# Causal mask of the by-query scores by 64x64 identities on four quarters of the array, and by-query scores one pair further ahead

## The chip, the cores and the metric

The kernel runs on one core of a Trainium2 chip. The metric is the device time of one execution in microseconds (us). "Before" is the median of three runs.

## What is computed

A batch of 16 sequences with 256 rows of 128 channels goes through two layers. Each has attention and a feed-forward part, and a layer norm behind each of the two. The change concerns the attention of the second layer:

```python
q = (x @ Wq).reshape(B, T, HEADS, D_K).transpose(0, 2, 1, 3)      # 16 heads of 8
k = (x @ Wk).reshape(B, T, HEADS, D_K).transpose(0, 2, 1, 3)
v = (x @ Wv).reshape(B, T, HEADS, D_V).transpose(0, 2, 1, 3)      # 64 per head
scores = jnp.einsum('bhqd,bhkd->bhqk', q, k) / scale
causal = jnp.triu(jnp.ones((T, T), dtype=bool), k=1)
scores = jnp.where(causal, -jnp.inf, scores)
attn = jax.nn.softmax(scores, axis=-1)
out = jnp.einsum('bhqk,bhkd->bhqd', attn, v) ... @ Wo
```

## The kernel before

The second layer (`l1_layer`) is one block in which each engine has its own program, a loop over `step(b)` for b from -4 to 17, unrolled. The engines meet only by semaphores. The order of the work in each program is written out by hand; each call such as `context(b, 0)` first waits for what it needs and then issues its instructions. The 16 heads of a sequence are handled as 8 pairs (`PRE = 8`); the two heads of a pair, u = 0 and 1, have their queries and keys on rows 0 to 63 and 64 to 127 of the stacks `q_ring` and `k_ring`.

Scores are computed twice. `scores_by_query(b, c)` puts queries on the partitions of the PSUM tensor `by_query` (one bank for each u), and VectorE's `maxima(b, c)` reduces them to the negated maximum of each query (L1375); after four pairs it combines them (L1380). `maxima_by_head` turns the maxima by two small transposes on TensorE, ScalarE's `maxima_out` copies them to `max_rows`, and SyncE's `rows_to_stack` writes them as one more row into `q_ring`, where they are subtracted by the matmul itself. `scores_by_key(b, c)` waits for that row at c = 0 and 4, and puts keys on the partitions of `by_key`. ScalarE's `exponential` makes probabilities of them (L1250), GpSimd's `mask` zeroes those above the diagonal (L1447), and `context` and `denominators` sum them on TensorE. `by_query` has room for one pair: `scores_by_query(b, c)` waits until `max_done` shows that the pair before it has been reduced.

Since the maximum must not see keys after the query, the by-query scores carry their own causal mask. Before the scores, a matmul with an identity of 128x128 adds a constant, `causal`, which holds -1e30 above the diagonal, to the two diagonal blocks of the bank (L1113). The scores follow with L1117 and L1121.

A step of TensorE has eight blocks, separated by blank lines in the code. Each has by-key scores of one pair, the context of the pair two before it, some other work (transposes of x, queries and keys, values, denominators, projections), and last by-query scores of the next sequence. I call them block 1 to block 8. The programs of ScalarE, VectorE and GpSimd follow the same rhythm. Names that matter here:

- `x_by_channel` (L1085), `queries_keys` (L1092), `values_of` (L1103), `maxima_by_head` (L1136), `context` (L1166), `denominators` (L1179) and `project` (L1190) on TensorE.
- `high_part` (L1263) on ScalarE: the first of three bf16 parts of queries and keys. `load_slots` (L113, L115) on SyncE copies the parts into the stacks, 12 loads a sequence, and `rows_to_stack` comes behind them in SyncE's queue.
- `reciprocals` (L1387), `add_attention`, `add_expert`, `second_input`, `third_input` (L1336) and `divide` (L1393) on VectorE. `second_input` waits for `root(pow2, ...)` on GpSimd, which waits for the statistics of `add_expert`.
- `root` (L1439, L1441), `low_part`, `gather` on GpSimd.

## Time and profile before

| | |
|---|---|
| median of 3 runs | 949.31 us (949.01, 949.31, 952.53) |
| profiled execution | 950.26 us, its span 948.5 us |
| TensorE clock granted, whole span | 0.937 |
| TensorE matmul, busy | 790.8 us, 83% of the span |
| VectorE / ScalarE / GpSimd, busy | 575.1 / 472.5 / 296.2 us |
| one step of the second layer, 605 to 631 us | TensorE 25.54 of 26.00 us, VectorE 17.75, ScalarE 12.87, GpSimd 10.91; granted clock 1.00 |

The second layer's scores run from about 406 to 811 us. Times are microseconds from the start of the span. A weight load (PEld) overlaps the matmuls (PE) of the same engine, and the ends of matmuls are modelled, so the recorded times of neighbours overlap.

### The profile page before, as it was taken

What the parts mean: (1) busy time and instruction counts of PE and PEld (TensorE: products, weight loads), DVE (VectorE), ACT (ScalarE), POOL (GpSimd) and SP (SyncE); (2) the same over time, 40 slices, a digit from 0 to 9 for tenths busy, and PEclk for the clock granted to TensorE, in tenths of its full rate; (3) what the DMA queues carried; (4) which work ended last, traced back from release to release, by engine and by line L of the source; (5) the groups of instructions that cost most, each with busy time, mean ns of one, the idle gap of its engine ahead of it and who ended that gap; (6) DMA issues with size and microseconds to landing.
All of it is one profiled execution on the core that took longest, in us unless ns stands there. A gap on an engine that the chain in (4) does not pass through costs nothing. (4 is left out here: it accounts for less than half of the span.)

```text
span 948.5 us, 19520 instructions
## 1 busy us (share of the span) xinstructions
PE 790.8 (83%) x7061; PEld 451.7 (48%) x7061; DVE 575.1 (61%) x1715; ACT 472.5 (50%) x750; POOL 296.2 (31%) x437
## 2 busy tenths in 40 slices
PE   1588989998829999179999999999999999739970
PEld 0234444444316778125555555555555555534430
DVE  4458999999531111244576776666666656324687
ACT  0377888887812222035454545445455444306664
POOL 3012333333336000424344444434443322100152
PEclk9989999999958999679999999999999999878995
DMA  0274333433215553221454444333334332210002
GB/s 26 72 239 124 97 89 96 108 84 89 69 32 129 158 149 88 67 59 45 96 96 96 96 96 92 74 86 78 81 76 96 79 85 51 56 45 0 1 0 89
DMA packets 111705, 78.02 MB, mean 82 GB/s; under 512 B 12272, under 2 KB 103088, under 8 KB 111616
## 3 DMA queue, kind: packets, MB, share of 16 engines
q1 hardware_dynamic: 107984, 71.16, 30.5%
q0 software_dynamic: 3344, 5.56, 2.2%
q8 instruction: 53, 0.87, 0.4%
q14 instruction: 36, 0.29, 0.1%
q10 hardware_dynamic: 288, 0.13, 0.1%
HBM read 37.86 MB, written 13.63 MB: 54 GB/s over the span
## 5 line engine op out<-in xcount | busy, mean ns | idle before, releaser
L1375 DVE TENSOR_REDUCE l_neg_max<-l_by_query 128x6 bf16<-128x768 f32 x128 | 122.5, 957 | 129.9 <-PE l_by_query L1121 129.6
L1447 POOL TENSOR_SCALAR_AFFINE_SELECT l_probs<-l_probs 128x512 f32<-128x512 f32 x128 | 87.1, 680 | 190.9 <-ACT l_probs L1250 190.7
L493 ACT ACTIVATE l_probs<-l_ps_s,minus_bound 128x1024 f32<-128x1024 f32 x128 | 137.9, 1116 | 2.3 <-PE l_ps_s L367 1.4
L1250 ACT ACTIVATE l_probs<-l_by_key 128x768 f32<-128x768 f32 x128 | 103.8, 811 | 68.1 <-PE l_by_key L1151 63.9
L1166 PE MATMUL l_ps_c<-l_probs,l_values 128*64 128x256 f32 (+1 forms) x1024 | 113.5, 343 | 0.0
L1166 PEld LDWEIGHTS l_ps_c<-l_probs,l_values 128*64 128x64 f32 x1024 | 62.9, 138 | 39.7 <-issue 21.2
L1190 PE MATMUL l_ps_v<-w_o,l_ctx 128*128 128x128 f32 x512 | 68.6, 290 | 15.1 <-DVE l_ctx L1393 15.1
L382 PE MATMUL l_ps_o<-l_probs,l_vpad 128*32 128x256 f32 x1024 | 80.6, 397 | 0.2
L1103 PE MATMUL l_ps_v<-w_v,l_xT 128*128 128x512 f32 x128 | 72.8, 651 | 0.4 <-ACT l_values L1271 0.2
L1190 PEld LDWEIGHTS l_ps_v<-w_o,l_ctx 128*128 128x128 f32 x512 | 62.6, 200 | 20.9 <-DVE l_ctx L1393 15.5
L1271 ACT ACTIVATE l_values<-l_ps_v 128x512 f32<-128x512 f32 x64 | 38.2, 597 | 65.4 <-PE l_ps_v L1103 60.0
L1393 DVE TENSOR_TENSOR l_ctx<-l_ctx,l_rrep 128x512 f32<-128x512 f32 x64 | 46.8, 774 | 23.9 <-DMA l_rrep<-rden_d 22.2
L1113 PE MATMUL l_by_query<-causal,ident_bf 128*128 128x256 bf16 x256 | 50.4, 279 | 12.2 <-DMA k_ring<-l_parts 10.0
L940 ACT ACTIVATE ex_hT<-ex_ps_h 128x640 f32<-128x640 f32 x32 | 22.5, 704 | 70.0 <-PE ex_ps_h L911 70.0
L1179 PE MATMUL l_ps_d<-l_probs,sums 128*32 128x256 f32 (+1 forms) x1024 | 55.1, 333 | 0.0
L367 PE MATMUL l_ps_s<-q_ring,k_ring 64*128 64x256 bf16 x512 | 51.5, 280 | 2.6 <-ACT l_probs L493 1.5
L1113 PEld LDWEIGHTS l_by_query<-causal,ident_bf 128*128 128x128 bf16 x256 | 21.6, 98 | 59.2 <-issue 33.2
L926 PE MATMUL ex_ps_y<-w,ex_hT 128*128 128x128 f32 (+1 forms) x384 | 48.9, 280 | 0.0
L776 POOL DMA_INDIRECT disp_d<-l_x,l_sidx x32 | 32.5, 1015 | 51.1 <-DVE weight L653 46.3
L926 PEld LDWEIGHTS ex_ps_y<-w,ex_hT 128*128 128x128 f32 (+1 forms) x384 | 43.4, 173 | 3.2 <-issue 0.2
L1277 ACT ACTIVATE l_ctx<-l_ps_c 128x512 f32<-128x512 f32 x64 | 38.2, 597 | 10.6 <-PE l_ps_c L1166 10.6
L911 PE MATMUL ex_ps_h<-ex_xeT,w 128*128 128x320 f32 x128 | 40.6, 463 | 1.3 <-DVE ex_xeT L960 0.7
(229 smaller groups left out, 1422.5 us busy)
## 6 DMA issues: line engine op xcount, KB each, us to landing
l_rrep<-rden_d SPq DMA_DIRECT2D x32, 512.0 KB
q_ring<-l_parts SPq DMA_DIRECT2D x192, 64.0 KB
k_ring<-l_parts SPq DMA_DIRECT2D x192, 64.0 KB
w<-in_L_ffn_w_dram SPq DMA_DIRECT2D x32, 256.0 KB, 3.0
disp_d<-zeros SPq DMA_DIRECT2D x8, 320.0 KB, 3.7
l_xin<-in_L_attn_x_dram SPq DMA_DIRECT2D x16, 128.0 KB, 3.1
l_xr<-in_L_attn_x_dram SPq DMA_DIRECT2D x16, 128.0 KB, 2.5
x_d<-l_x SPq DMA_DIRECT2D x16, 128.0 KB, 2.1
```

Source lines behind the costliest of these rows:

```text
L367: last = pe.matmul(ps_s[c % 2][:, g * N:(g + 1) * N], k_ring[i][half, 2 * j + e, kb * P:(kb + 1) * P], q_ring[i][half, 2 * j + e, :], star ...
L382: last = pe.matmul(ps_o[32 * g:32 * g + 32, t * N:(t + 1) * N], vpad[p][:, kb, f:f + 32], probs[c % RING][:, g * N:(g + 1) * N], start=u = ...
L493: act.activation(probs[c % RING][:, :], ps_s[c % 2][:, :], ACT.Exp, bias=k["minus_bound"][:, :], scale=SCALE).then_inc(probs_sb, 1)
L926: last = pe.matmul(ps_y[p][0:n, t // P * C:(t // P + 1) * C], hT[p][:, f, t:t + n], w2_sb[q][:, f, :], start=f == 0, stop=f == FC - 1)
L1103: pe.matmul(ps_v[:, :], xT[b % 2][:, j * P:(j + 1) * P], w_v[:, half * 512:(half + 1) * 512], start=True, stop=True).then_inc(v_ps, 1)
L1113: pe.matmul(by_query[:, u, P:3 * P], ident_bf[:, :], k["causal"][:, 0:2 * P], start=True, stop=False, skip_group_check=True)
L1166: last = pe.matmul(ps_c[u * DV:(u + 1) * DV, c % 2, q0:N], values[b % 2][:, kb, h * DV:(h + 1) * DV], pr[:, u, first:first + N - q0], star ...
L1179: last = pe.matmul(ps_d[32 * g:32 * g + 32, q0:N], sums[:, j, :], probs[(2 * j + e) % P_RING][:, u, first:first + N - q0], start=j == 0 an ...
L1190: last = pe.matmul(ps_v[:, j * C:(j + 1) * C], ctxs[b % 2][:, i, j * P:(j + 1) * P], w_o[:, i, :], start=i == 0, stop=i == PAIRS - 1)
L1250: act.activation(probs[c % P_RING][:, :, 0:N + P], by_key[:, :, 0:N + P], ACT.Exp, scale=SCALE).then_inc(p_sb, 1)
L1375: dve.tensor_reduce(neg_max[:, :, half, :, h].rearrange("p a u -> p u a"), by_query[:, :, 0:3 * P].rearrange("p u (a q) -> p u a q", a=3), ...
L1447: pool.affine_select(out=corners, in_=corners, compare_op=ALU.is_ge, fill=0.0, base=0, pattern=[[0, 4], [1, P]], channel_multiplier=-1).th ...
```

## The change

The constant `causal` becomes `corner`, 256 columns wide; each half of its partitions holds the first 64 rows of a causal block twice. The mask of a pair is now four matmuls, each with a 64x64 identity on its own quarter of the array. Two cover queries 0 to 63 of both diagonal blocks with 256 columns, one for each u; two cover queries 64 to 127, for which only keys 64 to 127 of a block need the mask, with 128 columns. The second two use the row half of the other u.

All by-query scores move one pair further ahead, in all programs: block 1 now does pair 2 of the next sequence where it did pair 1, and blocks 7 and 8 do pairs 0 and 1 of the one after. With them `x_by_channel` moves from the head of block 1 to behind its context, `maxima_by_head(b + 1, 0)` from block 5 to block 4, `high_part` behind `exponential(b, 4)`, and the work of VectorE and GpSimd is placed anew: on VectorE `add_expert` goes behind `maxima(b + 1, 4)` and `second_input` behind `maxima(b + 1, 5)`; on GpSimd `root(pow2, ...)` goes behind `mask(b, 6)` and `gather` behind `mask(b, 7)`.

```diff
-            pool.memset(k["causal"][:, :], 0.0).then_inc(filled, 1)
+            pool.memset(k["corner"][:, :], 0.0).then_inc(filled, 1)
...
-            pool.affine_select(out=k["causal"][:, :].rearrange("p (a b) -> p a b", b=P),
-                               in_=k["causal"][:, :].rearrange("p (a b) -> p a b", b=P),
-                               compare_op=ALU.is_ge, fill=-1e30,
-                               base=0, pattern=[[0, 4], [-1, P]], channel_multiplier=1).then_inc(cut, 1)
+            pool.wait_ge(cut, 2)
+            for half in range(2):
+                rows = k["corner"][64 * half:64 * half + 64, :].rearrange("p (a b) -> p a b", b=P)
+                pool.affine_select(out=rows, in_=rows, compare_op=ALU.is_ge, fill=-1e30,
+                                   base=0, pattern=[[0, 2], [-1, P]], channel_multiplier=1).then_inc(cut, 1)
...
                     for u in two:
-                        pe.matmul(by_query[:, u, P:3 * P], ident_bf[:, :], k["causal"][:, 0:2 * P],
+                        r = slice(64 * u, 64 * u + 64)
+                        pe.matmul(by_query[0:64, u, P:3 * P], ident_bf[r, r], k["corner"][r, :],
+                                  start=True, stop=False, skip_group_check=True)
+                    for u in two:
+                        r = slice(64 - 64 * u, 128 - 64 * u)
+                        later = by_query[64:128, u, P:3 * P].rearrange("p (a k) -> p a k", k=P)[:, :, 64:P]
+                        pe.matmul(later, ident_bf[r, r], k["corner"][r, :].rearrange("p (a k) -> p a k", k=P)[:, :, 0:64],
                                   start=True, stop=False, skip_group_check=True)
...
             def step(b):
-                x_by_channel(b + 2)
                 scores_by_key(b, 2)
                 context(b, 0)
-                scores_by_query(b + 1, 1)
+                x_by_channel(b + 2)
+                scores_by_query(b + 1, 2)
 
                 scores_by_key(b, 3)
                 context(b, 1)
                 denominators(b, 0)
                 queries_keys(b + 2)
-                scores_by_query(b + 1, 2)
+                scores_by_query(b + 1, 3)
 
                 scores_by_key(b, 4)
                 context(b, 2)
                 values_of(b + 1, 0)
-                scores_by_query(b + 1, 3)
+                scores_by_query(b + 1, 4)
 
                 scores_by_key(b, 5)
                 context(b, 3)
                 denominators(b, 1)
+                maxima_by_head(b + 1, 0)
                 values_of(b + 1, 1)
-                scores_by_query(b + 1, 4)
+                scores_by_query(b + 1, 5)
 
                 scores_by_key(b, 6)
                 context(b, 4)
-                maxima_by_head(b + 1, 0)
                 values_of(b + 1, 2)
-                scores_by_query(b + 1, 5)
+                scores_by_query(b + 1, 6)
 
                 scores_by_key(b, 7)
                 context(b, 5)
                 denominators(b, 2)
                 values_of(b + 1, 3)
-                scores_by_query(b + 1, 6)
+                scores_by_query(b + 1, 7)
 
                 scores_by_key(b + 1, 0)
                 context(b, 6)
                 project(b - 1, 0)
-                scores_by_query(b + 1, 7)
+                scores_by_query(b + 2, 0)
 
                 scores_by_key(b + 1, 1)
                 context(b, 7)
                 denominators(b, 3)
                 project(b - 1, 1)
                 maxima_by_head(b + 1, 1)
-                scores_by_query(b + 2, 0)
+                scores_by_query(b + 2, 1)
 
             steps(step)
 
                     act.activation(max_rows[half][:, :], turned, ACT.Copy).then_inc(rows_sb, 1)
 
             def step(b):
+                exponential(b, 2)
                 x_out(b + 2)
-                exponential(b, 2)
 
                 exponential(b, 3)
                 context_out(b, 0)
+
+                exponential(b, 4)
                 high_part(b + 2)
-
-                exponential(b, 4)
                 values_out(b + 1, 0)
 
                 exponential(b, 5)
                 context_out(b, 1)
+                maxima_out(b + 1, 0)
                 values_out(b + 1, 1)
 
                 exponential(b, 6)
-                maxima_out(b + 1, 0)
                 values_out(b + 1, 2)
 
                 exponential(b, 7)
 
             def step(b):
                 reciprocals(b - 1)
+                maxima(b + 1, 2)
+
                 add_attention(b - 2)
-                maxima(b + 1, 1)
+                maxima(b + 1, 3)
+
+                lower_parts(b + 2)
+                third_input(b - 2)
+                maxima(b + 1, 4)
 
                 add_expert(b + 3)
-                maxima(b + 1, 2)
-
-                third_input(b - 2)
-                lower_parts(b + 2)
-                maxima(b + 1, 3)
+                maxima(b + 1, 5)
 
                 second_input(b + 3)
-                maxima(b + 1, 4)
-
                 divide(b - 1, 0)
                 divide(b - 1, 1)
-                maxima(b + 1, 5)
+                maxima(b + 1, 6)
 
                 divide(b - 1, 2)
                 divide(b - 1, 3)
-                maxima(b + 1, 6)
-
                 maxima(b + 1, 7)
+
                 maxima(b + 2, 0)
+
+                maxima(b + 2, 1)
 
             steps(step)
 
 
             def step(b):
                 mask(b, 2)
+                mask(b, 3)
                 root(pow3, x3_step, (b - 2) * X3 + 1 + 2 * NB, mv3, veps3, rstd3, b - 2)
-                mask(b, 3)
-                root(pow2, x2_step, (b + 3) * X2 + 3 * NB, mv2, veps2, rstd2, b + 3)
                 mask(b, 4)
                 low_part(b + 2)
                 mask(b, 5)
+                mask(b, 6)
+                root(pow2, x2_step, (b + 3) * X2 + 3 * NB, mv2, veps2, rstd2, b + 3)
+                mask(b, 7)
                 gather(b + 4)
-                mask(b, 6)
-                mask(b, 7)
                 mask(b + 1, 0)
                 mask(b + 1, 1)
 
```

## Rows read from the trace of the kernel before

**Rows 1.** Line L1387 in 477 to 785 us: count, durations, first and last start.
```profile
L1387 DVE RECIPROCAL l_rden<-l_ps_d x13: 1747/1748/1750, 475.7 to 783.2; 128x256 f32<-128x256 f32 x13
```

**Rows 2.** Groups by line and form, 477 to 785 us: busy us, mean ns | idle before.
```profile
L1148 PEld LDWEIGHTS l_by_key<-q_ring,k_ring 64*128 64x128 bf16 x192 | 9.3, 94 | 8.2 <-DMA q_ring<-l_max_rows 5.5 <-issue 1.8
```

**Rows 3.** Waits of TensorE's matmuls, 470 to 790 us: total, times, longest.
```profile
PE l_by_query L1113 <- DVE l_neg_max L1375: 1.6, 2, 1.1
```

**Rows 4.** Timeline, step of 603 us: start, us, what [idle before <-releaser].
```profile
602.14 0.09 PEld L1136 LDWEIGHTS l_ps_m<-ident_bf,l_neg_max 128*8 128x8 bf16 x2
602.34 0.11 PEld L1113 LDWEIGHTS l_by_query<-causal,ident_bf 128*128 128x128 bf16 x2
...
602.94 0.20 PEld L1085 LDWEIGHTS l_ps_m<-ident,l_x 128*128 128x128 f32 x2 [0.16 <-issue]
...
603.58 0.87 PE L1166 MATMUL l_ps_c<-l_probs,l_values 128*64 128x256 f32 x8
...
604.38 0.11 PEld L1113 LDWEIGHTS l_by_query<-causal,ident_bf 128*128 128x128 bf16 x2 [0.17 <-issue]
...
604.71 0.10 PEld L1117 LDWEIGHTS l_by_query<-k_ring,q_ring 63*128 63x128 bf16 x2 [0.21 <-issue]
...
605.94 0.59 PEld L1179 LDWEIGHTS l_ps_d<-l_probs,sums 128*32 128x32 f32 x16 [0.17 <-issue]
```

**Rows 5.** Timeline of TensorE's matmuls, 612.5 to 614.3 us.
```profile
612.55 1.12 PE L1103 MATMUL l_ps_v<-w_v,l_xT 128*128 128x512 f32 x2
613.51 0.38 PE L1113 MATMUL l_by_query<-causal,ident_bf 128*128 128x256 bf16 x2
613.83 0.28 PE L1117 MATMUL l_by_query<-k_ring,q_ring 63*128 63x256 bf16 x2
...
614.00 0.27 PE L1148 MATMUL l_by_key<-q_ring,k_ring 64*128 64x256 bf16 x2
```

**Rows 6.** Timeline of the first two context matmuls at 603.58 us.
```profile
603.58 0.44 PE L1166 MATMUL l_ps_c<-l_probs,l_values 128*64 128x256 f32 x2
```

**Rows 7.** Matmuls by line and form, 477 to 785 us.
```profile
L1166 PE MATMUL l_ps_c<-l_probs,l_values 128*64 128x256 f32 x388 | 63.3, 405 | 0.0
```

**Rows 8.** Timeline of TensorE's matmuls, 616.6 to 621 us.
```profile
616.72 0.28 PE L1148 MATMUL l_by_key<-q_ring,k_ring 64*128 64x256 bf16 x2
...
619.97 0.22 PE L1121 MATMUL l_by_query<-k_ring,q_ring 63*128 63x128 bf16 x2
```

**Rows 9.** Timeline of ScalarE, 607 to 618 us.
```profile
607.90 0.60 ACT L1263 ACTIVATE l_parts<-l_ps_m 128x512 bf16<-128x512 f32 x1 [1.24 <-PE l_ps_m L1092]
...
608.56 0.81 ACT L1250 ACTIVATE l_probs<-l_by_key 128x768 f32<-128x768 f32 x1
...
617.10 0.81 ACT L1250 ACTIVATE l_probs<-l_by_key 128x768 f32<-128x768 f32 x1
```

**Rows 10.** Timeline of GpSimd, 609 to 618 us.
```profile
609.01 0.22 POOL L1439 TENSOR_SCALAR l_veps<-l_mv 128x2 f32<-128x2 f32 x1 [0.39 <-DVE l_mv L1330]
...
609.31 0.74 POOL L1441 TENSOR_TENSOR l_rstd<-l_veps,minus_half 128x2 f32<-128x2 f32 x1
...
617.97 0.64 POOL L1447 TENSOR_SCALAR_AFFINE_SELECT l_probs<-l_probs 128x512 f32<-128x512 f32 x1 [0.57 <-ACT l_probs L1250]
```

**Rows 11.** Timeline of VectorE, 391 us and 616 to 620 us.
```profile
391.85 0.60 DVE L1336 TENSOR_SCALAR l_x<-l_y,l_mv,l_rstd 128x128 f32<-128x128 f32 x2 [1.17 <-POOL l_rstd L1441]
...
616.21 1.74 DVE L1393 TENSOR_TENSOR l_ctx<-l_ctx,l_rrep 128x512 f32<-128x512 f32 x2 [1.03 <-DMA l_rrep<-rden_d]
617.87 0.95 DVE L1375 TENSOR_REDUCE l_neg_max<-l_by_query 128x6 bf16<-128x768 f32 x1
...
618.74 1.28 DVE L1393 TENSOR_TENSOR l_ctx<-l_ctx,l_rrep 128x512 f32<-128x512 f32 x2
```

**Rows 12.** Timeline of SyncE's issues: the first stack load of a step.
```profile
609.49 0.58 SPq L113 DMA_DIRECT2D q_ring<-l_parts  x1
```

**Rows 13.** Timeline at the layer's start: the first by-key scores.
```profile
421.70 0.28 PE L1148 MATMUL l_by_key<-q_ring,k_ring 64*128 64x256 bf16 x2 [2.13 <-DMA q_ring<-l_max_rows]
```

More of the change, by code:

```diff
@@ L178, in _ @@
             s.did(dve.tensor_copy(k["gate_T"][:, :], gps[:, :]))
-            dve.wait_ge(cut, 3)
+            dve.wait_ge(cut, 4)
             s.did(dve.tensor_copy(k["ident_bf"][:, :], k["ident"][:, :]))
@@ L1882, in program @@
             "tri_bf": sb("tri_bf", [P, P], BF16), "ones_bf": sb("ones_bf", [P, P], BF16),
-            "ones": sb("ones", [P, P], FP32), "causal": sb("causal", [P, 4 * P], BF16),
+            "ones": sb("ones", [P, P], FP32), "corner": sb("corner", [P, 2 * P], BF16),
             "zeros": sb("zeros", [P, 5 * C], FP32), "minus_half": sb("minus_half", [P, 4], FP32),
```

## The prediction, made before the change was run

> **What bounds the kernel now.** I read the page first, then the second layer alone: the waits of TensorE, the timeline of one step, and the same timeline for each other engine. The layer is a loop of 16 steps. The reciprocals, one a step, start from 475.7 to 783.2 us, 13 of them, so a step takes 307.5 / 12 = 25.63 us [rows 1]. TensorE works through all of it at a granted clock of 1.00, its upper level of 2.4 GHz (table above). Its only real idle times are the by-key scores that wait for the row of maxima in `q_ring`, 5.5 us in these 12 steps or 0.46 a step [rows 2], and two waits for a reduction of VectorE, 1.6 us together [rows 3]. (Most of what is booked before L1113 on the weight-load row is a load that waits while a matmul still streams, and costs nothing.) So the step is TensorE's instruction time, 25.17 us, plus 0.46 us of waiting; a microsecond on TensorE or in that wait is a microsecond of the kernel, 12 to 16 times over.
>
> Inside TensorE's time there is a second thing to see: the price of changing the tile shape. After the values' matmuls, which like the mask use the whole array, the first mask matmul starts at 613.51, 0.16 us before the recorded end of the work before it (612.55 + 1.12) [rows 5]. After the context's matmuls, whose tiles are 128x64, the mask's weight load starts at 604.38, only 0.07 us before their recorded end (603.58 + 0.87) [rows 4]. A change of shape thus drains the array: 0.10 us, with the exposed weight load 0.11. Every change shows it, also that from the transposes of 8 columns to the mask (0.20 us for two tiny matmuls, 602.14 to 602.34) and that from the by-query scores to the transposes of x (the 0.16 before 602.94) [rows 4].
>
> **The change on TensorE.** *The mask.* Today, after a change of shape, its two matmuls and the drain behind them take 604.38 to 604.71, 0.33 us [rows 4]. Four quarter matmuls are not in this trace, so I bound them. The nearest row is the context, whose two 128x64 tiles run at once: the first two matmuls are recorded with 0.44 us together, 0.43 each, the mean of that form is 0.405 over two such and two behind a hidden load, so the latter take 0.38 and a load of 64 columns shows for 0.05 [rows 6, 7]. A 256-column bf16 matmul streams for 0.11: the two of the mask take 613.51 to 613.83 with one drain of 0.10 in it [rows 5]. If the four quarters run together the mask takes 0.05 + 0.11 + 0.10 of drain = 0.26 us: 0.07 less, eight times a step, -0.56 us. Lower bound: no drain between 64x64 and the by-query scores' 64x128, 0.16 us. Upper bound: nothing overlaps, 0.32 of streaming + 0.15 = 0.47 us. I take 0.26, as for the context's tiles.
>
> The Trainium skill, "TensorEngine Tiling (Array Packing)", Key Properties, says that changing the tiling mode, not just the tile, drains the TensorE; the trace agrees with its 0.10 us. The same page, PSUM Pressure, says that different row tiles cannot access one PSUM bank simultaneously. Here each bank gets its second quarter from the other row half; by that rule the 128-column quarters come after the 256-column ones, which is the third case below.
>
> *The changes of shape.* In blocks 2 to 7 of a step the mask follows values, projections or queries and keys, all on the whole array, with no change of shape. With 64x64 tiles each gains one: 6 x 0.11. In block 8 the transposes before it drain already: no new one. In block 1 the transposes of x no longer stand between by-query and by-key scores, which have one shape, but between context and mask: two changes go, one comes, -0.11. Together +0.54 us a step. So what the mask saves (-0.56) the drains take back: 0.0 us a step, and this is the core of the forecast. The half-size constant and the one more select at the start move tenths of a microsecond, once.
>
> **The change in the order.** Everything VectorE and GpSimd do for TensorE must be placed again. I follow one step from T, the first by-key matmul of block 5.
>
> TensorE: blocks 5 and 6 take 614.00 to 620.02 today (by-key follows the by-query matmuls of 619.97 at once) [rows 5, 8], 6.02 us. The transposes of the maxima leave block 5 for block 4 (-0.20 [rows 4]), two changes of shape less two shorter masks come (+0.08): 5.90. Mask and scores of pair 7 are the last 0.26 + 0.18 of it, so TensorE asks for `max_done` of pair 6 at T + 5.46.
>
> The other engines: pair 6's reduction now stands behind `second_input` and two `divide`s, `second_input` behind `root(pow2)` on GpSimd, and that behind `mask(b, 6)`. By-key to exponential 0.38 (616.72 to 617.10), exponential 0.81, hand-over 0.06, mask 0.64 [rows 8, 9, 10]; root 1.04 (609.01 to 610.05) and a hand-over, 1.09 [rows 10]: T + 2.98. Two normalisations take 0.60 (391.85) where GpSimd runs nothing beside them, as here: 3.6. Two `divide`s with a mask beside them, as `mask(b, 7)` will be, 1.74 (616.21), alone 1.28 (618.74); I take 1.7: 5.3. The reduction 0.95 and a hand-over 0.05 [rows 11]: T + 6.3. TensorE waits **0.8 us** (0.4 if the `divide`s run alone, 1.2 if the normalisations too lose 0.4 to a mask). Today `second_input` runs two blocks after its statistics and no such chain ends at TensorE. Behind the waiting mask are queued the by-key scores of the next batch's pair 0, and with them ScalarE and GpSimd; `divide` 2 and 3 end at about T + 7.7, before the projection asks at T + 7.8.
>
> This wait does not add to the wait for the row; it covers it. That row is issued behind 12 stack loads, which SyncE begins at 609.49 [rows 12], and those wait for the high part. `high_part` now comes after exponential 4: 608.56 + 0.81 + 0.60 [rows 9], less 0.13 that TensorE is earlier there, is 609.84, where today it is there before 609.49. So the row is 0 to 0.4 us later (less where a load is held by the queue anyway). The earlier transposes of the maxima don't help: it is SyncE's queue that is late, not `max_rows`. The wait of a step becomes the larger of 0.8 and 0.46 + (0 to 0.4); as the row's own wait spreads from 0 to over 1 us, I take 0.92 for the mean. That is +0.46 us in the 12 steps which have all of the chain: **+5.5 us**.
>
> Other moves: gather goes behind `mask(b, 7)` and so past two masks on GpSimd; its two issues are done by T + 7.3, `mask(b + 1, 0)` can't start before T + 7.9, and the rows are used a third of a step later. `add_attention` one block later still ends before block 3's scores need it, the lower parts end over 1 us before `max_done` of pair 4 is asked for. The two waits of [rows 3] fall in step 14, where the reciprocal stood before pair 1's reduction and no longer does, and in step 12: **-1.6 us**. At the layer's start the first row of maxima already sets the by-key scores (2.13 us of idle at 421.70) [rows 13], and queries and keys of batch 1, hence its stack loads, now stand behind one more by-query pair and its reduction: 0.95 for the reduction and, as an estimate, the pair's 0.44 to 0.88 at full or half clock with a hand-over, less one pair that is then done: **+1.5 us** (0 to 2).
>
> **Sum.** 0 + 5.5 - 1.6 + 1.5 = +5.4 us. The profiled execution took 950.26 us (span 948.5, 1.8 around it), so 955.7; the runs' median of 949.31 is 0.95 less, so 954.7. I say 955.0, +0.6%. 0.5% (4.7 us) is about what a measurement of this kernel tells from no change.
>
> **Rivals.**
> *Order neutral.* If mask and `divide` are not in each other's way (0.4 in place of 0.8) and the queue absorbs the later high part, the wait stays near 0.46: 0 - 1.6 + 1.5, about 949.5. For it: in some steps the stack loads' issues are stretched already, and a later start costs them nothing. Against: the chain is ten instructions with known durations, and its sum must fall by 0.4 us in every step.
> *Quarters apart* (the page's bank rule as mechanism of this kernel): the 128-column quarters follow the others, +0.053 us x 128 pairs = +6.8: 961.5; with nothing overlapped, +0.21 x 128 = +27. For it: no row shows four quarters, nor two row halves on one bank. Against: the tiles of one column half each overlap here (0.44 for the first two).
> *Faster: no drain behind the quarters.* The by-query scores use 64 rows too; if only a change of row tiling drains, 0.10 x 128 = -12.3 us: 942.5. It decides as soon as half of the pairs skip it. Against: from the context's 128x64 to the denominators' 128x32 the rows don't change either, and the load there idles 0.17 all the same (605.94) [rows 4].
>
> **Chances.** Forecast 0.45 (951 to 959, of it 0.12 below 954.05), order neutral 0.25, quarters apart 0.18, no drain 0.12. Hence faster 0.12, same 0.38, slower 0.50. The range leaves out most of "no drain" and the dear end of "quarters apart": 945 to 965.
>
> **What would show it.** L1113's successor: four matmuls a pair that start within 0.02 us, and 0.26 us to the by-query load, both before and after which the weight-load row idles 0.16 to 0.2. Idle before the mask of pair 7 "until DVE l_neg_max" of some 0.8 us in steps 1 to 12; by-key waits for `max_rows` down to 0.1 to 0.2 a step. Reciprocals about 26.1 us apart. The prediction is wrong if the reciprocals are 25.6 or less apart, if the mask takes over 0.3 us or under 0.2, or if pair 7 doesn't wait.

## The result: +0.42%, and the profile after

The changed kernel takes **951.74 us** (median of 20 runs, 947.92 to 959.58), the kernel before 948.10 us on the same chip (20 runs, 943.57 to 952.53). The ratio is 1.0042 [1.0022, 1.0062]: slower, by a little less than the 0.5% that I had set as the bound of no change, and within the range of 945 to 965. The profiled execution took 954.15 us, its span is 952.4 us. Two executions, one of the kernel before at 1140.78 us (granted clock 0.65) and one of kernel 8 below at 1445.4 us (granted clock 1.00), are far slower than all others and left out of the ratios; no run explains them.

The page of the changed kernel, its summary of TensorE and its groups of the mask and the by-key scores:

```profile
span 952.4 us, 20034 instructions
...
PE 785.1 (82%) x7317; PEld 447.4 (47%) x7317; DVE 569.5 (60%) x1715; ACT 472.0 (50%) x750; POOL 312.8 (33%) x438
...
L1115 PE MATMUL l_by_query<-corner,ident_bf 64*64 64x256 bf16 x256 | 38.8, 300 | 14.8 <-DMA k_ring<-l_parts 10.1
...
L1155 PE MATMUL l_by_key<-q_ring,k_ring 64*128 64x256 bf16 x256 | 35.8, 276 | 12.9 <-DMA q_ring<-l_max_rows 12.4
```

TensorE is busy for 5.7 us less than before and the span is 3.9 us longer: it works less and waits more. The line numbers have moved by up to 8: the mask is L1115 and L1120 (before L1113), the by-key scores are L1155 and L1158, the reduction L1382, the reciprocals L1394.

The reciprocals of the changed kernel (one line's instructions, 13 starts), and then the by-key weight load in the same 12 steps (groups by line and form):

```profile
L1394 DVE RECIPROCAL l_rden<-l_ps_d x13: 1745/1747/1748, 480.6 to 790.3; 128x256 f32<-128x256 f32 x13
```

```profile
L1155 PEld LDWEIGHTS l_by_key<-q_ring,k_ring 64*128 64x128 bf16 x192 | 9.3, 94 | 10.9 <-DMA q_ring<-l_max_rows 9.9
```

A step is 309.7 / 12 = 25.81 us, 0.18 more than in [rows 1], and the idle time for the row of maxima has gone from the 5.5 us of [rows 2] to 9.9. The waits of TensorE's matmuls in these steps (total, times, longest) answer to [rows 3]:

```profile
PE l_by_key L1155 <- DMA q_ring<-l_max_rows: 7.3, 10, 1.1
PE l_by_query L1115 <- DVE l_neg_max L1382: 1.7, 8, 0.2
```

The second of them is new in its place: it stands before the mask of pair 7, in 11 of the 12 steps (the view has eight of them; three are too short for it). A recorded idle time counts only what lies behind the modelled end of the matmul before it. I therefore also added up, from the starts of all TensorE instructions in these 12 steps, how far each start lies behind what the same pair of instructions needs without a wait. By that count the waits of a step were 0.40 us before and are 0.93 now, and the rest of a step, TensorE's own work, was 25.23 and is 24.87. The table further down uses this count.

The mask, from the timeline of the matmuls and weight loads after a block of projections:

```profile
603.83 0.72 PE L1197 MATMUL l_ps_v<-w_o,l_ctx 128*128 128x128 f32 x5
604.49 0.30 PE L1115 MATMUL l_by_query<-corner,ident_bf 64*64 64x256 bf16 x2
604.49 0.24 PE L1120 MATMUL l_by_query<-corner,ident_bf 64*64 64x128 bf16 x2
604.72 0.28 PE L1124 MATMUL l_by_query<-k_ring,q_ring 63*128 63x256 bf16 x2
```

```profile
604.48 0.11 PEld L1115 LDWEIGHTS l_by_query<-corner,ident_bf 64*64 64x64 bf16 x2
604.49 0.11 PEld L1120 LDWEIGHTS l_by_query<-corner,ident_bf 64*64 64x64 bf16 x2
604.71 0.10 PEld L1124 LDWEIGHTS l_by_query<-k_ring,q_ring 63*128 63x128 bf16 x2
```

All four quarters start within 0.01 us, although two row halves write different columns of each bank. From the mask's load to the by-query scores' load it is 0.23 us (0.33 in [rows 4]). The load at 604.48 starts 0.07 us before the recorded end of the projections (604.55), as it did at a change of shape in [rows 4]: the drain ahead of the mask is there.

The chain that ends at the mask of pair 7, each engine's own timeline of one step, T = 620.40:

```profile
620.40 0.27 PE L1155 MATMUL l_by_key<-q_ring,k_ring 64*128 64x256 bf16 x2
...
620.77 0.81 ACT L1257 ACTIVATE l_probs<-l_by_key 128x768 f32<-128x768 f32 x1
...
621.65 0.64 POOL L1455 TENSOR_SCALAR_AFFINE_SELECT l_probs<-l_probs 128x512 f32<-128x512 f32 x1 [2.45 <-ACT l_probs L1257]
622.25 0.22 POOL L1447 TENSOR_SCALAR l_veps<-l_mv 128x2 f32<-128x2 f32 x1
622.56 0.71 POOL L1449 TENSOR_TENSOR l_rstd<-l_veps,minus_half 128x2 f32<-128x2 f32 x1
624.17 1.50 POOL L1455 TENSOR_SCALAR_AFFINE_SELECT l_probs<-l_probs 128x512 f32<-128x512 f32 x1 [0.91 <-ACT l_probs L1257]
...
623.37 0.60 DVE L1343 TENSOR_SCALAR l_x<-l_y,l_mv,l_rstd 128x128 f32<-128x128 f32 x2 [1.65 <-POOL l_rstd L1449]
623.89 1.29 DVE L1400 TENSOR_TENSOR l_ctx<-l_ctx,l_rrep 128x512 f32<-128x512 f32 x2
625.10 0.96 DVE L1382 TENSOR_REDUCE l_neg_max<-l_by_query 128x6 bf16<-128x768 f32 x1
...
626.11 0.30 PE L1115 MATMUL l_by_query<-corner,ident_bf 64*64 64x256 bf16 x2 [0.21 <-DVE l_neg_max L1382]
...
627.79 0.28 PE L1155 MATMUL l_by_key<-q_ring,k_ring 64*128 64x256 bf16 x2 [1.12 <-DMA q_ring<-l_max_rows]
```

The mask that ran beside the first two `divide`s of [rows 11] in the kernel before, on GpSimd:

```profile
616.37 1.03 POOL L1447 TENSOR_SCALAR_AFFINE_SELECT l_probs<-l_probs 128x512 f32<-128x512 f32 x1
```

`second_input` starts at T + 2.97, the reduction at T + 4.70, the mask at T + 5.71. A load that follows a drain starts 0.07 us before the recorded end of the work before it; here it starts 0.21 behind it. So the wait is 0.28 us here; it is 0.21 to 0.29 us in 11 of the 12 steps, 0.24 us a step in the mean. Right behind the scores that follow it, the by-key scores wait for the row as well, 1.12 us here.

SyncE's issues in that step, and the first by-key scores of the layer:

```profile
616.22 0.58 SPq L113 DMA_DIRECT2D q_ring<-l_parts  x1
...
625.38 1.32 SPq L1045 DMA_DIRECT2D q_ring<-l_max_rows  x2
```

```profile
426.24 0.30 PE L1155 MATMUL l_by_key<-q_ring,k_ring 64*128 64x256 bf16 x2 [2.51 <-DMA q_ring<-l_max_rows]
```

The first stack load starts 5.81 us after the reciprocal of its step (VectorE, 610.41); the one of [rows 12] started 5.56 after its own (603.93). From the first by-query scores of the layer to the first by-key scores it was 15.94 us and is 17.97 (2.13 of idle time in [rows 13], 2.51 now). From the 14th reciprocal of the layer, the last of the 13 above, to its 16th and last it was 43.78 us and is 41.02.

So of the +3.90 us in the span, the 12 steps give +2.10, the layer's start +2.43 (2.04 up to the first by-key scores, 0.39 from there to the second reciprocal), its last two steps -2.76, and what follows the 16th reciprocal -0.38. The other +2.51 lies ahead of the code that was changed: the second layer's first by-query scores start at 408.3 us instead of 405.8. In the first 263 us the granted clock was 0.99 before and is 0.97 now. Over all the kernels below, whose first layer is the same, that start lies anywhere between 405.8 and 410.5, and the profile of the kernel before happens to have the earliest.

### The profile page after: what moved, and what is told of

The parts are those of the page before. It is cut to its first block and busy times, and to the rows that moved or that the text cites. A ratio compares the mean times of both kernels' runs of the same rounds, so it can differ in the third digit from the quotient of the medians.

```text
span 952.4 us, 20034 instructions
## 1 busy us (share of the span) xinstructions
PE 785.1 (82%) x7317; PEld 447.4 (47%) x7317; DVE 569.5 (60%) x1715; ACT 472.0 (50%) x750; POOL 312.8 (33%) x438
## 3 DMA queue, kind: packets, MB, share of 16 engines
q0 software_dynamic: 3344, 5.56, 2.2%
## 5 line engine op out<-in xcount | busy, mean ns | idle before, releaser
L1382 DVE TENSOR_REDUCE l_neg_max<-l_by_query 128x6 bf16<-128x768 f32 x128 | 121.7, 951 | 116.7 <-PE l_by_query L1128 116.5
L1455 POOL TENSOR_SCALAR_AFFINE_SELECT l_probs<-l_probs 128x512 f32<-128x512 f32 x128 | 92.6, 724 | 187.2 <-ACT l_probs L1257 187.0
L1197 PEld LDWEIGHTS l_ps_v<-w_o,l_ctx 128*128 128x128 f32 x512 | 63.3, 202 | 21.0 <-DVE l_ctx L1400 15.6
L1115 PE MATMUL l_by_query<-corner,ident_bf 64*64 64x256 bf16 x256 | 38.8, 300 | 14.8 <-DMA k_ring<-l_parts 10.1
L1115 PEld LDWEIGHTS l_by_query<-corner,ident_bf 64*64 64x64 bf16 x256 | 13.8, 104 | 78.0 <-DVE l_neg_max L1382 38.3
L1400 DVE TENSOR_TENSOR l_ctx<-l_ctx,l_rrep 128x512 f32<-128x512 f32 x64 | 41.8, 696 | 13.5 <-DMA l_rrep<-rden_d 13.5
L1465 POOL DMA_INDIRECT l_eg<-eout_d,l_index x32 | 44.1, 1377 | 9.5 <-issue 4.9
L1155 PE MATMUL l_by_key<-q_ring,k_ring 64*128 64x256 bf16 x256 | 35.8, 276 | 12.9 <-DMA q_ring<-l_max_rows 12.4
```

What stands on the lines that cost most here:

```text
L1115: pe.matmul(by_query[0:64, u, P:3 * P], ident_bf[r, r], k["corner"][r, :], start=True, stop=False, skip_group_check=True)
L1197: last = pe.matmul(ps_v[:, j * C:(j + 1) * C], ctxs[b % 2][:, i, j * P:(j + 1) * P], w_o[:, i, :], start=i == 0, stop=i == PAIRS - 1)
L1382: dve.tensor_reduce(neg_max[:, :, half, :, h].rearrange("p a u -> p u a"), by_query[:, :, 0:3 * P].rearrange("p u (a q) -> p u a q", a=3), ...
L1455: pool.affine_select(out=corners, in_=corners, compare_op=ALU.is_ge, fill=0.0, base=0, pattern=[[0, 4], [1, P]], channel_multiplier=-1).th ...
```

## The experiments

All ratios are to the kernel before, run on the same chip, with 95% intervals. "Step" is the distance of the reciprocals as in [rows 1], "waits" and "own work" are the count explained above, per step, each from one profiled execution (the 0.1 us of a weight load that stands bare behind a wait is in the own work); "to the first by-key" is measured from the first by-query scores of the layer.

| kernel | ratio | span | step | waits (row / pair 7) | own work | to the first by-key |
|---|---|---|---|---|---|---|
| before | 1 | 948.5 | 25.63 | 0.40 (0.33 / 0) | 25.23 | 15.9 |
| after | 1.0042 [1.0022, 1.0062] | 952.4 | 25.81 | 0.93 (0.68 / 0.24) | 24.87 | 18.0 |
| 1 mask alone | 1.0001 [0.9977, 1.0026] | 948.5 | 25.58 | 0.53 (0.41 / 0) | 25.06 | 15.6 |
| 2 order alone | 1.0051 [1.0028, 1.0073] | 950.3 | 25.67 | 0.66 (0.40 / 0.25) | 25.01 | 18.6 |
| 3 second quarters on the same rows | one time, 961.59 us | 959.9 | 26.18 | 1.07 (0.80 / 0.24) | 25.12 | 17.9 |
| 4 high part back | 1.0024 [0.9998, 1.0050] | 950.2 | 25.80 | 0.82 (0.55 / 0.24) | 24.98 | 17.9 |
| 5 root first | 1.0097 [1.0063, 1.0131] | 953.5 | 25.83 | 0.83 (0.81 / 0) | 24.99 | 17.8 |
| 6 row early, before | 0.9923 [0.9898, 0.9949] | 940.1 | 25.15 | 0.02 (0 / 0) | 25.14 | 14.7 |
| 7 row early, after | 0.9944 [0.9921, 0.9967] | 943.6 | 25.12 | 0.32 (0.07 / 0.24) | 24.79 | 16.5 |
| 8 row early, root first, after | 0.9914 [0.9891, 0.9937] | 941.1 | 24.88 | 0.07 (0.06 / 0) | 24.81 | 16.5 |
| 9 tall mask, before | 0.9973 [0.9951, 0.9996] | 944.2 | 25.41 | 0.81 (0.63 / 0) | 24.60 | 15.5 |
| 10 tall mask, row early, before | 0.9868 [0.9836, 0.9900] | 935.1 | 24.83 | 0.31 (0.13 / 0) | 24.53 | 14.2 |
| 11 tall mask, row early, root first, after | 0.9857 [0.9834, 0.9880] | 935.1 | 24.52 | 0.19 (0.04 / 0) | 24.32 | 16.5 |
| 12 row sent twice, before | one time, 993.91 us | 992.2 | 28.64 | 2.47 (2.33 / 0) | 26.17 | 18.2 |

### 1 and 2. The two halves of the change

The first kernel has the mask and its constant as changed and every program in the order of before; the second has the mask of before and the new order.

```diff
# 1: the kernel before, with
+                        pe.matmul(by_query[0:64, u, P:3 * P], ident_bf[r, r], k["corner"][r, :],
...
# 2: the changed kernel, with
+                        pe.matmul(by_query[:, u, P:3 * P], ident_bf[:, :], k["causal"][:, 0:2 * P],
```

> The order of before, with the mask by four quarters. My theory (the mask itself saves a little on TensorE, the new order loses it in waits): in blocks 1 and 8 the mask and its drain go from 0.33 to 0.23 us, in the six others the added drain eats it (+0.01), so TensorE's work is 0.14 us a step shorter; what of it lies before the by-key scores of pair 0 goes into their wait for the row of maxima. Ratio 0.998 to 1.000, steps about 25.6 us apart, row waits 0.4 to 0.5 us a step. Rival (the added changes of tile shape are what costs): slower by 2 us or more, ratio above 1.002.

> The new order with the mask of before, 128x128 identity. My theory: the row of maxima is later because the stack loads begin later, some 0.8 us of wait a step against 0.4 to 0.5, plus 0.1 to 0.3 us before the mask of pair 7, plus 2 us at the start of the layer: ratio 1.003 to 1.007. Rival (the order is neutral or gains, and the mask costs): ratio 0.997 to 1.001.

The mask alone changes nothing that can be measured: 948.41 us, 1.0001. Eight masks save 0.10 us each and six new changes of shape take most of that back; TensorE's own work falls by 0.17 us a step. But waits take its place: the by-key scores wait for the row 0.08 us a step more, and the transposes of x 0.11. These wait for ScalarE's copy of the turned maxima, `maxima_out` (`rows_sb` in the code of `x_by_channel`). The timeline of the mask alone, and behind it the same copy in the kernel before:

```profile
603.70 0.37 ACT L1290 ACTIVATE l_max_rows<-l_ps_m 8x256 bf16<-8x256 bf16 x1 [2.37 <-PE l_ps_m L1143]
603.95 0.22 PE L1128 MATMUL l_by_query<-k_ring,q_ring 63*128 63x128 bf16 x2
604.19 0.20 PEld L1086 LDWEIGHTS l_ps_m<-ident,l_x 128*128 128x128 f32 x2 [0.26 <-issue]
```

```profile
602.45 0.37 ACT L1283 ACTIVATE l_max_rows<-l_ps_m 8x256 bf16<-8x256 bf16 x1 [2.37 <-PE l_ps_m L1136]
```

In both kernels the transposes' load starts 0.11 to 0.12 us after the copy's end (604.07 and 602.82), as in every step from 560 to 700 us. In the new order it starts 1.0 to 1.1 us after it, and this wait is gone.

The order alone has all of the cost: 953.32 us, 1.0051. Its wait before pair 7 is the 0.25 us a step of the full change, and its start is as late (18.6 us). One part of what I expected did not come: the waits for the row are 0.40 us a step, not 0.8. Its profiled step is only 0.04 us longer and its span 1.8, so the profile shows less than half of the 4.8 us in the ratio. The rest is not shown. A lower clock is not what the record points to: the mean granted clock of its 12 executions is 0.937, of the 28 of the kernel before on the same chip 0.935.

### 3. Do two row halves on one bank wait for each other?

```diff
-                        r = slice(64 - 64 * u, 128 - 64 * u)
+                        r = slice(64 * u, 64 * u + 64)
```

> After, with the second quarters on the same row half as the first quarter of their bank (each PSUM bank is written from one row half). If crossing the row halves mattered in the changed kernel, its four matmuls would start in two groups there and together here or the other way round; since there they start within 0.01 us, I expect no difference: 0.23 us from the mask's first load to the by-query load, 948 to 954 us. Rival (two quarters in one row half share a path and run one after the other): 0.28 us or more a pair, 7 us more.

Now each bank is written by one row half only, which computes the same. The mask is no shorter (timeline, after a wait for pair 6):

```profile
681.18 0.30 PE L1115 MATMUL l_by_query<-corner,ident_bf 64*64 64x256 bf16 x2 [0.21 <-DVE l_neg_max L1382]
681.19 0.24 PE L1120 MATMUL l_by_query<-corner,ident_bf 64*64 64x128 bf16 x2
681.41 0.28 PE L1124 MATMUL l_by_query<-k_ring,q_ring 63*128 63x256 bf16 x2
```

0.23 us from mask to scores, and the quarters 0.01 apart, as in the changed kernel. "Quarters apart" is refuted in both its forms: neither the row halves nor the four quarters are in each other's way. The Trainium skill, "TensorEngine Tiling (Array Packing)", PSUM Pressure, says that different row tiles cannot access the same PSUM bank simultaneously; in the changed kernel two row tiles write different partitions and columns of one bank at the same time, and no time is lost. The one time of this kernel, 961.59, is long for another reason: two of its steps took 28.6 and 28.3 us, with the lower clock behind waits for the row of 1.86 and 1.42 us (see 12), and its layer starts latest of all, at 410.5 us.

### 4. The high part and SyncE's queue

```diff
+                high_part(b + 2)
                 exponential(b, 4)
-                high_part(b + 2)
```

> After, with high_part ahead of exponential(b, 4) again. My theory (a later high part starts the stack loads 0.25 us later and with them the row): first load 3.8 us after the reciprocals instead of 4.1, row waits down by 0.2 us a step at most, since the queue stretches some issues anyway: 1 to 3 us less than after, ratio 1.001 to 1.004. Rival (the loads' start doesn't matter): as after, 1.003 to 1.006, row waits as before.

In the steps where nothing else holds it, the first stack load comes 0.25 us earlier again (5.56 us after the reciprocal for 5.81), and the counted waits for the row fall from 0.68 to 0.55 us a step. But in other steps the load starts up to 7.6 us after the reciprocal, and in the mean of the 12 steps the row is issued 14.19 us after it, for 14.20 in the changed kernel. So this run does not show that the queue hands the high part's delay on. 951.12 us, 1.0024 with an interval that holds both 1 and the changed kernel's 1.0042: the effect on the time is not settled either.

### 5. The wait before pair 7, taken away

```diff
+                root(pow2, x2_step, (b + 3) * X2 + 3 * NB, mv2, veps2, rstd2, b + 3)
                 mask(b, 6)
-                root(pow2, x2_step, (b + 3) * X2 + 3 * NB, mv2, veps2, rstd2, b + 3)
                 mask(b, 7)
```

> After, with root(pow2) ahead of mask(b, 6) on GpSimd. My theory (the wait of 0.28 us before the mask of pair 7 ends a chain mask, root, second_input, two divides, reduction; but behind it the row of maxima is late anyway): that wait goes to 0 in all 12 steps, the row waits grow by the same, from 8.2 to about 11 us in 12 steps, and the time stays: ratio to before 1.003 to 1.006. Rival (the chain is what costs): 3 us less than after, ratio 1.000 to 1.002.

The wait is gone from every step, and the kernel is slower, 957.35 us. What pair 7 no longer waits, the by-key scores right behind it wait for the row, 0.81 us a step instead of 0.68: the two waits cover each other, as forecast, so removing the first gains nothing. That explains "no faster" and not the +5 us, which neither my theory nor the rival had. The timeline of one step and its stretches (columns: stretch, length, busy time of PE, PEld, DVE, ACT, POOL, granted clock, DMA share, GB/s) show something else:

```profile
627.64 0.28 PE L1155 MATMUL l_by_key<-q_ring,k_ring 64*128 64x256 bf16 x2 [1.89 <-DMA q_ring<-l_max_rows]
627.76 0.22 PE L1158 MATMUL l_by_key<-q_ring,k_ring 64*128 64x128 bf16 x2
627.91 0.87 PE L1173 MATMUL l_ps_c<-l_probs,l_values 128*64 128x256 f32 x8
628.71 3.34 PE L1197 MATMUL l_ps_v<-w_o,l_ctx 128*128 128x128 f32 x16
...
634.48 2.05 PE L1197 MATMUL l_ps_v<-w_o,l_ctx 128*128 128x128 f32 x16
```

```profile
616.00:625.00 9.00, 9.00 (x101) 4.43 (x100) 8.54 (x19) 5.78 (x9) 4.51 (x8) 1.00 0.81 171
625.00:627.60 2.60, 0.75 (x9) 0.23 (x8) 1.68 (x3) 0.60 (x1) 1.86 (x2) 1.00 0.20 52
627.60:632.50 4.90, 4.86 (x34) 3.91 (x36) 0.00 (x0) 0.81 (x1) 0.63 (x1) 0.67 0.07 17
632.50:641.00 8.50, 8.50 (x109) 5.65 (x106) 4.68 (x5) 4.38 (x7) 1.91 (x3) 0.99 0.03 9
```

After a wait of 1.89 us TensorE's granted clock is 0.67 for some 5 us, a mean of its upper level (2.4 GHz) and its lower one (1.2 GHz), and 16 projection matmuls take 3.34 us instead of 2.05. That step took 28.4 us. It is the only such step of this profile, and the mean step is as long as in the changed kernel (25.83 and 25.81). The mean granted clock of the kernel's 7 executions is 0.932, of the 20 of the kernel before on the same chip 0.936. This fits more such falls in the other executions, but that they make the +5 us is argued and not shown.

### 6, 7 and 8. The row out of the queue

SyncE sends the first row of maxima of a sequence before the last two of its twelve stack loads:

```diff
                     load_slots(sp, 1, parts[b % 2], q_ring[i], k_ring[i], stacks_in[i])
+                if real(b + 1):
+                    rows_to_stack(b + 1, 0)
+                if real(b + 2):
                     sp.wait_ge(lo_sb, b + 3)
                     load_slots(sp, 2, parts[b % 2], q_ring[i], k_ring[i], stacks_in[i])
                 if real(b + 1):
-                    rows_to_stack(b + 1, 0)
                     rows_to_stack(b + 1, 1)
```

6 is the kernel before with it, 7 the changed kernel with it, 8 is 7 with the root first, as in 5.

> Before, with one thing changed: SyncE issues the first row of maxima ahead of the last two stack loads and their wait for the third bf16 part. My theory (the row waits in SyncE's queue behind the stack loads): the issue is 1.3 us earlier or more, the row waits of 0.4 to 0.5 us a step go to near 0, 4 to 6 us less, ratio 0.994 to 0.996. Rival (the row's own transfer or the transposes are late): no change, ratio 0.999 to 1.001, waits as before.

> After, with the same one change in SyncE's queue. My theory: the 0.8 to 0.9 us of row wait in each of 12 steps go nearly all, and about 1.3 us of the late start of the layer; what is left is the wait of 0.28 us before the mask of pair 7. 10 us less than after, ratio to before 0.991 to 0.995, steps about 25.0 us apart. Rival (another wait, on VectorE or on the stacks, takes the place of it): ratio near 1.00 to 1.004.

> The changed kernel with the first row of maxima sent ahead of the low-part load, and the root of the combination ahead of GpSimd's mask of pair 6. With the row early there is no longer a row wait that the removed wait could fall into. Theory (the 0.28 us wait for pair 7's divides is on the path once the row is out of the way): it goes, 12 to 14 of them, and the time is some 3 us under that of the changed kernel with the row early alone: 0.990 to 0.992 of before. Rival (the wait only moves again, to the row or to ScalarE's exponentials): no better than 0.994. The kernel has no wait of about 2 us for the row, so its times should lie close together (within 5 us).

SyncE's timeline in 7 shows the row leave where stack loads stood:

```profile
617.83 0.60 SPq L115 DMA_DIRECT2D k_ring<-l_parts  x1
618.48 1.32 SPq L1045 DMA_DIRECT2D q_ring<-l_max_rows  x2
619.84 0.60 SPq L113 DMA_DIRECT2D q_ring<-l_parts  x1
```

In 6 the row is issued 1.3 us earlier, its wait is gone from the steps and the layer's start is 1.3 us shorter (14.7 for 15.9); this is more than the 4 to 6 us that I expected. The early row is worth 0.8% in the kernel before and 1.0% in the changed one. With the row early a step of 7 is as long as one of 6 (25.12 and 25.15): what TensorE saves, 0.35 us, stands as 0.24 us before pair 7 and 0.07 for the row. 7 is 0.2% behind 6 (943.85 and 941.98 us), about the 1.8 us of the later start. Only in 8, where no wait for the row takes over what it saves, does the root's move pay: 0.24 us a step, 0.9914. The edit that cost 0.5% in 5 gains some 0.3% here (the intervals of 7 and 8 overlap, the steps are 25.12 and 24.88).

### 9, 10 and 11. A mask without a change of shape

Here the mask uses 64 rows and all 128 columns, like the by-query scores behind it. `other_bf` is the identity with its column halves swapped; the first matmul of a bank puts the block of 64 queries in its place, the second adds the other.

```diff
+            turns = (ident_bf, k["other_bf"])
...
+                        r = slice(64 * u, 64 * u + 64)
+                        pe.matmul(by_query[:, u, P:3 * P], turns[u][r, :], k["corner"][r, :],
+                                  start=True, stop=False, skip_group_check=True)
...
+                        later = by_query[:, u, P:3 * P].rearrange("p (a k) -> p a k", k=P)[:, :, 64:P]
+                        pe.matmul(later, turns[1 - u][r, :], k["corner"][r, :].rearrange("p (a k) -> p a k", k=P)[:, :, 0:64],
+                                  start=False, stop=False, skip_group_check=True)
```

> The kernel before with the 64x128 mask alone; nothing else is changed, the row is sent late as before. The early row was worth 0.008 of before alone, both together 0.013. Theory A (TensorE's own work bounds the step outside the row wait, so a mask without drains shortens the step by what it saves): TensorE's work falls by some 0.6 us a step but the late row takes part of it back, time 0.992 to 0.998. Theory B (the late row sets the step): 0.999 or more, and all of the saving stands as waits for the row, with times spread over 8 us or more.

> The order of before with the early row of rows_early_before, and the mask by 64x128 tiles, the shape of the by-query scores that follow: for each u its own row half adds queries 0 to 63 with 256 columns and then queries 64 to 127 with 128 columns. My theory (the drain behind the mask is paid for the change of tile shape alone): no idle of 0.2 us before the by-query load any more, mask to scores 0.17 us in place of 0.33; TensorE's work in a step 0.5 to 0.6 us shorter than in rows_early_before, which has no waits left: 6 to 9 us less, ratio to before 0.983 to 0.987. Rival (a drain is due before the scores anyway, or another wait appears): ratio 0.990 to 0.995.

> The same, with the mask as 64x128 matmuls (64 rows by all 128 columns) in the place of the 64x64 quarters. With the order of before and the early row this mask gave 0.987 of before. Theory (mask form and order are separate terms; the order costs its layer start of some 2 us and gives back as much at the end): 0.983 to 0.988. Rival (without the slack of the quarters' drain the pair-7 chain or the x transposes become the wait): 0.989 or more.

Weight loads of 10 on the timeline:

```profile
604.74 0.10 PEld L1125 LDWEIGHTS l_by_query<-corner,other_bf 64*128 64x128 bf16 x1
604.75 0.10 PEld L1125 LDWEIGHTS l_by_query<-corner,ident_bf 64*128 64x128 bf16 x1
604.85 0.10 PEld L1129 LDWEIGHTS l_by_query<-k_ring,q_ring 63*128 63x128 bf16 x2
```

```profile
604.73 0.28 PE L1120 MATMUL l_by_query<-corner,ident_bf 64*128 64x256 bf16 x1
...
604.91 0.28 PE L1129 MATMUL l_by_query<-k_ring,q_ring 63*128 63x256 bf16 x2
```

From mask to scores it is 0.18 us on the matmuls, against 0.23 for the quarters, and there is no drain at the scores: the next loads run on while the mask streams. TensorE's own work is 0.63 us a step less than before (9), against 0.17 for the quarters (1). Alone it gives 0.27%, since the row's wait rises to 0.63 us a step and that of the transposes of x by 0.16. With the row early the two together give 1.3%, of which the mask has some 0.55% (10 beside 6). In the new order with row and root first all together give 1.4%, the mask again some 0.55% of it (11 beside 8). The intervals of 10 and 11 overlap: the order is worth nothing that can be measured. 10 and 11 beat both kernels, and 10 does it without the new order.

### 12. The row, 2 us later

The kernel before, with the first row of each sequence sent twice; the by-key scores wait for the second.

```diff
+                for again in range(2 - half):
+                    if again:
+                        sp.wait_ge(rows_in[half], b * 64 + 32)
                     for u in two:
```

> The kernel before with the first row of maxima of each sequence sent twice, the second time after the first has landed; by-key pair 0 waits for the second. This makes the row some 2 us later in each of 12 to 14 steps and changes no other instruction. Theory A (a wait costs its own length and no more): steps of about 27.6 us instead of 25.7, a span of 972 to 980 us, granted clock of TensorE as before. Theory B (after a wait of TensorE of 2 us or more the chip grants it the lower clock for some us): steps of 28.5 us and more, a lower clock behind each such wait, a span of 990 us or more and a mean granted clock under 0.92.

Two steps of it on TensorE's timeline, and the stretch behind a third wait:

```profile
556.49 0.28 PE L1151 MATMUL l_by_key<-q_ring,k_ring 64*128 64x256 bf16 x2 [2.28 <-DMA q_ring<-l_max_rows]
...
557.56 2.05 PE L1193 MATMUL l_ps_v<-w_o,l_ctx 128*128 128x128 f32 x16
...
584.20 0.28 PE L1151 MATMUL l_by_key<-q_ring,k_ring 64*128 64x256 bf16 x2 [2.38 <-DMA q_ring<-l_max_rows]
...
585.27 3.40 PE L1193 MATMUL l_ps_v<-w_o,l_ctx 128*128 128x128 f32 x16
```

```profile
613.60:620.00 6.40, 6.37 (x36) 4.83 (x38) 0.00 (x0) 0.81 (x1) 0.64 (x1) 0.51 0.00 0
```

The wait is 2.0 us a step longer (2.33 for 0.33), and a step is 3.0 us longer. The missing 0.94 is TensorE's own work at the lower clock, 0.51 behind the wait at 613.6. Theory B holds for the time (28.64 a step, 992.2 us) with a mean clock of 0.922, a little over what was expected. But not every such wait is followed by the lower clock. Over the profiles of all 14 kernels, from 480 to 860 us, none of 73 recorded waits for the row of up to 1.29 us was; of 17 between 1.42 and 2.84 us, 10 were and 7 were not, the longest of these 2.58. What decides it no run here shows. The page's mean clock of an execution goes with its time too: over the 20 runs of the changed kernel the five fastest had 0.937 on average, the five slowest 0.931. This alone does not point to the row: 6, which has no wait for it in the steps, has 0.939 in its three fastest and 0.935 in its three slowest, and the kernel before 0.936 and 0.933 in the five fastest and slowest of 28.

## Why the prediction was right, and where only in the sum

955.0 us was forecast and 951.74 measured; +0.6% and +0.42%. None of the three signs of being wrong came: steps of 25.81 us, a mask of 0.23 us, and a wait before pair 7. By its own steps:

- **The mask**, 0.26 us forecast, 0.23 measured (0.33 before). If streaming and drain are as forecast (0.11 and 0.10), the exposed load of a 64-column weight is the term that was too large: the 0.05 read off the context's fp32 tiles is about 0.02 here. Times eight, that is the first part of the miss.
- **The changes of shape**: they came as forecast, both before and behind the quarters, and take back most of the mask's saving. Forecast for TensorE's own work: 0.0 a step; measured -0.36, of which the mask alone has -0.17 (1) and the order alone -0.22 (2). In the timeline of 2 the order saves at two places: 0.22 us where the transposes of x stand behind the context (forecast -0.11; part of it may be the wait for `maxima_out`, which is gone), and 0.12 us where the transposes of the maxima follow the denominators and no longer the context (forecast as a move that saves nothing). That is more than -0.22 because the bare weight loads behind the waits count as own work. The 0.16 us before 602.94 in [rows 4], read as a drain, is thus no clean proof of one: that load stands 0.12 us behind the end of the copy. "What the mask saves the drains take back" was half right.
- **The wait before pair 7**: forecast 0.8, measured 0.28. The chain is right to 0.01 us up to `second_input` (T + 2.98 and T + 2.97), and TensorE's readiness to 0.03 (626.11 less 0.28 is T + 5.43, forecast 5.46). The failed term is the two `divide`s, 1.7 forecast and 1.29 measured; another 0.16 us is that the recorded times of neighbours on VectorE overlap by 0.08 each, which the sum adds up in full. I took the 1.74 us of [rows 11], where a mask runs beside them. Here GpSimd's mask pays instead, with 1.50 us for 0.64; nobody waits for it. The Trainium skill, "GPSIMD Engine Reference", Specifications, names this contention with GpSimd for VectorE instructions with two SBUF inputs, which a `divide` has; both traces agree. The times of the single instructions fit one that stands while the other runs: before, the mask ends 0.49 us behind the first `divide` (616.91 and 617.40) and the second `divide` takes 1.11 us instead of 0.68; now both `divide`s take 0.69 and the mask ends 0.50 us behind the second (625.18 and 625.68). Why the mask came between the two in one case and not in the other, no run here explains.
- **The row**: forecast to be 0 to 0.4 us later because of the high part, and 0.25 is what the first stack load shows. Its wait rises by 0.35 us a step. Counted from the reciprocal of its step, in the mean of the 12, SyncE issues the row at 13.87 us before and at 14.20 now, 0.33 later, and TensorE is ready for it at 16.16 and 16.06, the wait before pair 7 included, 0.10 earlier. That the high part is what makes the row late is not shown: with it back (4) the row is issued at 14.19, and with the mask alone (1), where the programs of ScalarE and SyncE are those of before, at 14.06. Forecast for all waits of a step: 0.92; counted: 0.93. That this sum agrees is luck in part: the row has the larger share of it, where pair 7 was to have it.
- **A step** is thus +0.18 us, not +0.46: the waits' growth (+0.53, forecast +0.46) less TensorE's saving (-0.36), which I had at nothing. This term alone is 3.3 of the 5.4 us.
- **Start and end**: +2.43 (forecast 1.5, 0 to 2) and -2.76 in the last two steps (forecast -1.6). Of the two waits behind the -1.6, one, 0.55 us at 748.40, lies within the 12 steps; only the other, 1.08 us at 786.97, is in the last two. The other 1.7 us there were not forecast, and no run explains them.
- **Slips in the sums**: 6 x 0.11 less 0.11 is 0.55 and not 0.54, 0.10 x 128 is 12.8 and not 12.3, and the neutral order comes to 949.2 and not 949.5. They change nothing.

From these terms the changed kernel would be 2.10 + 2.43 - 2.76 - 0.38 = +1.4 us, and +3.9 with the later start of the whole layer, which varies from execution to execution; the medians differ by 3.6. So the total came nearer than its terms, and that is luck in part too. Longer waits for the row, some of them long enough to be followed by the lower clock, could give the difference between 1.4 and 3.6, and 5 and 12 show that mechanism. The profiled execution of the changed kernel has no such fall in its steps, and only profiled executions have a trace, so for its other runs this is argued and not shown.

Of the rivals, "quarters apart" is refuted by the after profile and by 3. "No drain behind the quarters" did not happen, but 9 shows its mechanism in another form: with columns that match the scores, half the rows alone make no change of shape. "Order neutral" had one of its premises right (the `divide`s run at 1.3) and the other open (what the queue hands on), and its result is refuted by 2: the order alone costs 0.5%.

## What to carry to other kernels

Ask of every TensorE saving which wait will absorb it. Here one edit cost 0.5% with the row late in SyncE's queue and with it early gained some 0.3%, which is not clear of noise in the times but stands in the steps as 0.24 us; so mend the last wait of a step before counting cycles in front of it. When packing small matmuls, match the shape of their neighbours rather than use more of the array: the 64x128 mask beat the 64x64 quarters because it needed no drain. A wait near 2 us on TensorE may cost half as much again in clock (12: 2.0 us more of wait, 3.0 us more of step), and a chain that shortens one wait by lengthening another can lose by it.

## What the hardware showed that I had not expected

- TensorE's granted clock fell from its upper to its lower level for some 5 us after 10 of 17 waits for the row of 1.42 to 2.84 us, and after none of 73 shorter ones; 16 projection matmuls then took up to 3.78 us instead of 2.05.
- Two row halves wrote different partitions and columns of one PSUM bank at once, at no cost: quarters 0.01 us apart, 0.23 us in all, the same as with one row half for each bank.
- Two `divide`s of VectorE beside a mask of GpSimd lost about the same in all, but not on the same engine: `divide`s 1.74 and mask 1.03 us before (GpSimd at 616.37), `divide`s 1.29 and mask 1.50 after; the two sums are 2.77 and 2.79. The times of the single instructions fit one that stands until the other is done.
